# The last 48 columns of a routed expert's gated activations: rounded part and rest in one stationary tile

## The reference

```python
x = L0_attn_x                       # (4, 512, 256), f32
xn = _layernorm(x, axis=-1)
# experts: E, H, TOP_K = (8, 176, 2), ROUTED_SCALE = 2.5, xt = xn as rows
scores = jax.nn.sigmoid(xt @ gate_w.T)
top_scores, top_idx = jax.lax.top_k(scores, TOP_K)
top_scores = top_scores / (jnp.sum(top_scores, axis=-1, keepdims=True) + 1e-20) * ROUTED_SCALE
h = jnp.einsum('td,edh->eth', xt, w1)
u = jnp.einsum('td,edh->eth', xt, w3)
y = jnp.einsum('eth,ehd->etd', jax.nn.silu(h) * u, w2)
routed = jnp.einsum('etd,te->td', y, combine)       # combine: the two chosen scores of a row
shared = jax.nn.silu(xt @ sw1) * (xt @ sw3) @ sw2
x = x + attention(xn, wq, w_down, w_up, wo) + (routed + shared)
```

## Time and profile before

| | us |
|---|---|
| median of 3 runs | 741.92 |
| lowest, highest | 740.95, 744.02 |
| the profiled execution | 740.12 |
| its span, first to last instruction | 738.2 |

### The profile page before, as it was taken

One profiled execution on the slowest core, in us unless ns is written; L12 is line 12 of the kernel. 1 busy time (PEld: TensorE's weight loads), 2 busy tenths in 40 slices (PEclk: granted clock), 3 DMA queues, 4 the chain that ended last, 5 costly groups with the idle time before them and its releaser, 6 DMA issues.

```text
span 738.2 us, 15624 instructions
## 1 busy us (share of the span) xinstructions
PE 699.8 (95%) x4554; PEld 629.4 (85%) x4554; DVE 633.0 (86%) x1724; ACT 592.9 (80%) x1472; POOL 540.0 (73%) x497
## 2 busy tenths in 40 slices
PE   4788979999999999999999999999999999999985
PEld 3677777898898999999999999999999999988875
DVE  6677989999998889888988888898889888888885
ACT  3666667888878898888888888888888888888872
POOL 2544457788777778788888878787887788786890
PEclk9999999999999999999999999999999999999999
DMA  9552522443333455656456654655566545512103
GB/s 300 166 166 98 206 62 100 132 161 115 117 118 133 130 150 138 184 135 164 124 157 175 165 128 131 197 150 139 130 159 174 149 133 144 133 13 61 58 9 107
DMA packets 64899, 99.85 MB, mean 135 GB/s; under 512 B 9472, under 2 KB 38320, under 8 KB 64816
## 3 DMA queue, kind: packets, MB, share of 16 engines
q1 hardware_dynamic: 57664, 89.52, 39.1%
q0 software_dynamic: 7152, 9.34, 7.6%
HBM read 70.06 MB, written 28.78 MB: 134 GB/s over the span
## 4 chain that ended last, share of the span: by engine, by line
PE 71%; DVE 14%; ACT 5%; issue 4%; POOL 4%; DMA 1%; DVEq 0%; ACTq 0%; POOLq 0%
PE qk_proj L453 14%; PE u_acc L453 13%; PE scores L453 12%; PE ffn L453 10%; PE out_acc L453 10%; PE probs_t L556 7%; DVE acc L1261 2%; ACT swapped L768 2%; DVE rot L1206 2%; POOL rot L928 2%; POOL swapped L920 2%; DVE rot L1213 2%; DVE pt_lo L1237 1%; PE ffn L637 1%; PE ffn L611 1%
## 5 line engine op out<-in xcount | busy, mean ns | idle before, releaser
L920 POOL TENSOR_TENSOR swapped<-swapped,sin_t 128x512 f32<-128x512 f32 x128 | 167.7, 1310 | 140.8 <-DVE rot L1213 109.3
L935 POOL TENSOR_TENSOR qk_lo<-rot,qk_hi 128x512 fp32r<-128x512 f32 x128 | 163.3, 1295 | 8.5 <-ACT qk_hi L777 8.1
L1237 DVE TENSOR_TENSOR pt_lo<-probs_t,pt_hi 128x512 fp32r<-128x512 f32 x238 | 117.6, 494 | 48.7 <-ACT pt_hi L799 48.5
L788 ACT ACTIVATE probs<-scores,nbias 128x512 f32<-128x512 f32 (+3 forms) x256 | 135.1, 528 | 28.3 <-DVE nbias L1222 26.8
L768 ACT ACTIVATE swapped<-qk_proj 64x512 f32<-64x512 f32 x256 | 151.9, 593 | 6.1 <-PE qk_proj L453 1.4
L799 ACT ACTIVATE pt_hi<-probs_t 128x512 fp32r<-128x512 f32 x238 | 104.9, 441 | 42.8 <-PE probs_t L556 34.2
L1222 DVE CUSTOM_DVE_ANT_0 scores<-scores,mask 128x512 f32<-128x512 f32 (+3 forms) x256 | 125.2, 489 | 7.8 <-PE scores L453 1.5
L1261 DVE SCALAR_TENSOR_TENSOR acc<-out_acc,rsum,acc 128x256 f32<-128x256 f32 x256 | 111.0, 475 | 3.6 <-PE out_acc L453 1.8
L556 PE MATMUL probs_t<-ident,probs 128*128 128x128 f32 x604 | 105.4, 273 | 6.7 <-DVE pt_lo L1237 6.5
L1206 DVE TENSOR_TENSOR rot<-qk_proj,cos_t 128x512 f32<-128x512 f32 x128 | 87.4, 683 | 10.0 <-ACT swapped L768 9.2
L556 PEld LDWEIGHTS probs_t<-ident,probs 128*128 128x128 f32 x604 | 75.5, 140 | 22.5 <-issue 7.0
(11 more groups left out here) (181 smaller groups left out, 1907.8 us busy)
## 6 DMA issues: line engine op xcount, KB each, us to landing
wt<-expert_parts SPq DMA_DIRECT2D x39, 704.0 KB, 4.5
wt<-expert_parts SPq DMA_DIRECT2D x39, 512.0 KB, 3.9
raw_a<-in_attn SPq DMA_DIRECT2D x8, 768.0 KB, 5.2
xs_sorted<-u_lo SPq DMA_DIRECT2D x3, 1677.0 KB, 9.5
xs<-xs_sorted SPq DMA_DIRECT2D x39, 129.0 KB, 2.6
expert_parts<-split SPq DMA_DIRECT2D x8, 352.0 KB, 2.4
expert_parts<-raw_f SPq DMA_DIRECT2D x8, 352.0 KB, 2.4
ys_tokens<-mask SPq DMA_DIRECT2D x1, 2176.0 KB, 7.5
```

The costliest lines, as they stand in the source:

```text
L788: ac.activation(probs[:, m % 2, PR_AT[i]:PR_AT[i] + n], s_bank[i % 2][:, 0:n], ACT.Exp, bias=nbias[:, m % 2, i:i + 1], scale=-1.0, accum_o ...
L920: pool.tensor_tensor(swapped[:, which, :], swapped[:, which, :], sin_t[:, :], ALU.mult).then_inc(sinm_ok[which], 1)
L935: pool.tensor_tensor(qk_lo[:, m % 2, which, :], rot[:, which, :], f32(qk_hi[:, m % 2, which, :]), ALU.subtract).then_inc(rlo_ok[which], 1)
L1237: ve.tensor_tensor(pt_lo[:, c], turn_bank(m, j)[:, 0:n], f32(pt_hi[:, c]), ALU.subtract).then_inc(ptlo_ok, 1)
```

## The change

For routed tiles alone the second chunk is packed. VectorE writes the last 48 columns of g twice, to columns 128 to 175 and again to 192 to 239, so that after the transposes rows 0 to 47 and rows 64 to 111 hold the same values. ScalarE writes g_hi's second chunk only in rows 64 to 127; its rows 0 to 63 are cleared once by GpSimd before the first routed tile. VectorE's subtraction, which is the same instruction as before, then leaves in g_lo's second chunk the value itself (rounded on being written, as hi would be) in rows 0 to 63 and the rest in rows 64 to 127. The weights' last 48 rows are loaded twice too, to rows 0 to 47 and 64 to 111. One pass over the packed tile with the rounded weights gives hi x hi and lo x hi, a second with the weights' rests gives hi x lo, and in addition lo x lo. Five passes take the place of six; shared tiles keep six. ScalarE waits for GpSimd's clearing at the first routed tile, GpSimd for the last shared tile's output before it clears.

```diff
--- before.py
+++ after.py
@@ -43,6 +43,8 @@
 UP = 2 * HID
 W13, W2C = KD * UP, 2 * D
 FCOLS = W13 + W2C
+
+REST, HALF = HID - P, P // 2
 PART = [slice(0, W13), slice(W13, FCOLS)]
 
 F32 = mybir.dt.float32
@@ -254,7 +256,7 @@
         RAW_DMAS = [0]
         for e in (E, *range(E)):
             RAW_DMAS.append(RAW_DMAS[-1] + 2 * len(cuts(e * HID, HID, 2 * P)))
-            RAW_DMAS.append(RAW_DMAS[-1] + sum(len(cuts(e * HID + n, m, P)) for n, m in ((0, P), (P, HID - P))))
+            RAW_DMAS.append(RAW_DMAS[-1] + sum(n * len(cuts(e * HID + a, m, P)) for n, a, m in ((1, 0, P), (2, P, REST))))
         RAW_DMAS = RAW_DMAS[2:]
 
         def part_steps(s):
@@ -316,7 +318,9 @@
                     first, rows = e * HID + c * P, min(P, HID - c * P)
                     for a, z in cuts(first, rows, P):
                         src = ffn_d[a // (2 * P)][a % P:a % P + z - a, W2 + a // P % 2 * D:W2 + a // P % 2 * D + D]
-                        sp.dma_start(raw_f[a - first:z - first, W13 + c * D:W13 + c * D + D], src).then_inc(ld_raw, 16)
+                        for row in (0, HALF)[:c + 1]:
+                            sp.dma_start(raw_f[row + a - first:row + z - first, W13 + c * D:W13 + c * D + D],
+                                         src).then_inc(ld_raw, 16)
 
             for b in range(B):
                 sp.dma_start(acc[:, NT * b:NT * b + NT, :],
@@ -644,9 +648,17 @@
                 pe.wait_ge(glo_ok, f + 1)
                 if t is not None:
                     pe.wait_ge(ld_w2, 16 * (t + 1))
-                w = [(wt[:, 0, W13 + c * D:W13 + c * D + D], wt[:, 1, W13 + c * D:W13 + c * D + D]) for c in range(2)]
-                x = [(g_hi[:, c * P:c * P + P], g_lo[:, c * P:c * P + P]) for c in range(2)]
-                product(f_bank[:, 0:D], list(zip(x, w)), True, True).then_inc(y_ok, 1)
+                if t is None:
+                    w = [(wt[:, 0, W13 + c * D:W13 + c * D + D], wt[:, 1, W13 + c * D:W13 + c * D + D]) for c in range(2)]
+                    x = [(g_hi[:, c * P:c * P + P], g_lo[:, c * P:c * P + P]) for c in range(2)]
+                    product(f_bank[:, 0:D], list(zip(x, w)), True, True).then_inc(y_ok, 1)
+                    return
+                w = [wt[:, i, W13:W13 + D] for i in range(2)]
+                product(f_bank[:, 0:D], [((g_hi[:, 0:P], g_lo[:, 0:P]), w)], True, False)
+
+                pe.matmul(f_bank[:, 0:D], g_lo[:, P:2 * P], wt[:, 0, W13 + D:FCOLS], start=False, stop=False)
+                pe.matmul(f_bank[:, 0:D], g_lo[:, P:2 * P], wt[:, 1, W13 + D:FCOLS], start=False,
+                          stop=True).then_inc(y_ok, 1)
 
             def batch_rows(s):
                 b = pro_batch(s)
@@ -825,7 +837,13 @@
                     return
                 need(ac, y_ok, f)
                 ac.wait_ge(gt_ok, f + 1)
-                ac.activation(g_hi[:, :], f_bank[:, 0:2 * P], ACT.Copy).then_inc(ghi_ok, 1)
+                if routed(f) is None:
+                    ac.activation(g_hi[:, :], f_bank[:, 0:2 * P], ACT.Copy).then_inc(ghi_ok, 1)
+                    return
+                if routed(f) == 0:
+                    ac.wait_ge(zero_ok, 4)
+                ac.activation(g_hi[:, 0:P], f_bank[:, 0:P], ACT.Copy)
+                ac.activation(g_hi[HALF:P, P:2 * P], f_bank[HALF:P, P:2 * P], ACT.Copy).then_inc(ghi_ok, 1)
 
             def result(f):
                 t = routed(f)
@@ -1007,6 +1025,10 @@
                     scatter(n)
                 result_home(ffn_tile(s - 1))
                 row_homes(ffn_tile(s + 1))
+                if s == GAPS[-1]:
+
+                    pool.wait_ge(y_ok, STILES)
+                    pool.memset(g_hi[0:HALF, P:2 * P].bitcast(U32), 0).then_inc(zero_ok, 1)
                 for group in ADDS.get(s, ()):
                     add_routed(group, s)
                 if s == -LEAD + 1:
@@ -1288,12 +1310,18 @@
                     return
                 ve.wait_ge(gated_ok, f + 1)
                 need(ve, gt_ok, f)
-                ve.tensor_tensor(g[:, 0:HID], gated[:, :], f_bank[:, HID:UP], ALU.mult).then_inc(g_ok, 1)
+                last = ve.tensor_tensor(g[:, 0:HID], gated[:, :], f_bank[:, HID:UP], ALU.mult)
+
+                if routed(f) is not None:
+                    last = ve.tensor_tensor(g[:, P + HALF:P + HALF + REST], gated[:, P:HID],
+                                            f_bank[:, HID + P:UP], ALU.mult)
+                last.then_inc(g_ok, 1)
 
             def g_parts(f):
                 if f is None:
                     return
                 ve.wait_ge(ghi_ok, f + 1)
+
                 ve.tensor_tensor(g_lo[:, :], f_bank[:, 0:2 * P], f32(g_hi[:, :]), ALU.subtract).then_inc(glo_ok, 1)
 
             def add_shared(f):
```

## The result

The changed kernel takes 736.84 us (median of 4 runs, 735.76 to 738.02), the kernel before in the same comparison 741.43 us. The ratio is 0.9932, with a 95% interval of 0.9918 to 0.9946: 0.7% faster. The forecast was 737.2 us, 4.68 us less than the kernel before; measured are 4.59 us less. The profiled execution has 736.77 us and a span of 734.9, against 740.12 and 738.2 before.

What follows compares the result with a forecast made beforehand. PE was taken to bind, full in the routed stretch; 39 removed passes at 0.120 us give 4.68 us, all additions counted as 0, so the median of 741.92 becomes 737.2 us. The range for 8 in 10 was 735.0 to 740.5.

Steps and rivals of the forecast that it cites:

- The price of the pass: PE's output passes in 39 routed tiles: one pass fewer, at 0.120 us each, gains 4.68 us.
- PE's stretch is full: PE from 240 to 650 us: busy throughout, no wait, all steps 10.56 us long, to become 10.44.
- VectorE's second product: 48-column product in each routed tile: 0.13 us (bounds 0 to 0.26), covered by PE margins of 0.68 us and more.
- ScalarE's two copies: g_hi copy split in two per routed tile: 0.32 us, 0.06 more (bounds 0 to 0.26), covered by idle time.
- rival A: Added slots reach PE in steps with extra work, its stretch is less full, or loads late: 739.6 to 741.9 us; chance 0.15.
- GpSimd and SyncE: One clearing at step 14 and 11 further DMAs of up to 48 KB: both taken as cost 0.
- Rival B: VectorE's added product delays u_lo past out_acc in routed steps, from 0.69 us added; 3.9 us slower, 745.8; chance 0.04.
- Rival C: On PE, the removed pass is worth its whole 0.283 us: 11.0 us gained, 730.9 us; chance 0.03.
- The signs: Wrong if PE waits for u_lo, g or rot, routed steps aren't 0.12 us shorter, or time before 235 us moves over 1.

Runs made afterwards that it cites:

- The halves exchanged: Changed kernel with ScalarE writing the rounded values to rows 0 to 63 of g_hi's second chunk, the other half cleared; ratio 0.9926, median 736.60 us.
- the additions alone: Changed kernel with the last pass issued twice in routed tiles, so six passes again; ratio 0.9996, routed stretch 405.80 us.
- the pass alone: Kernel before with one output pass left out in each routed tile and nothing added; ratio 0.9943, routed stretch 401.24 us.

## Why the prediction was right, step by step

**The price of the pass** held to the last digit: 0.120 us from the chain, 38 x 0.12 = 4.56 in the run that removes it alone. The twelve passes beside it in the earlier trace rows were the right scale, and so was setting the 0.283 us of the earlier trace rows aside. The Trainium skill's sustained spacings ("TensorE: Matmul & The Clock Gate", Back-to-back issue gap), 81 ns at 128 columns and 131 ns at 512, give an estimated 98 ns at 256 when drawn in a straight line (the prediction took 95), which would have made 3.7 us for the 38; this case has 4.56.

**PE's stretch is full.** In plain steps no wait, one step length, and each 0.12 us removed shortens the step by 0.12, down to 9.97: shown. The steps with attention weights were 11.42 us long already before; the prediction gave one length for all.

**VectorE's second product**: 0.12 us, taken as 0.13, covered. The margin to the transposes of g was read right in kind and too large by 0.13: 0.55 us of cover where I had 0.68. What I had wrong is the way of the delay. I read the stretch from 410.35 to 413.28 as one without a gap and let all behind the product come 0.13 later; but pt_lo had waited there for pt_hi, and u_lo and g_lo come no later than before. For the same reason the idle time ahead of the later pt_lo is 0.80 us in the changed kernel, not the 0.69 that was to show it.

**ScalarE's two copies are the step that failed.** I took 0.32 us from the slot of a 128-column copy and they hold the engine for 0.59, with qk_hi longer by 0.13 in the steps where pt_hi follows at once: 0.45 us in place of 0.06. The term was mis-sized: the slot of 0.16 was that of two operations that both start at partition 0, and the bounds of 0 and 0.26 did not hold it. Nor did I list the wait that it reaches. In the step with attention weights pt_hi doesn't stand idle, it follows its queue; VectorE's pt_lo comes right after it and PE's next transposes after that. In the kernel before, pt_lo ended at 275.81 us, and the weight load of these transposes started at 276.29: 0.48 us. Take off 0.45 on ScalarE, 0.12 because PE is there a pass sooner, and the 0.05 from an end to a start, and the load is 0.14 us late: about the 0.12 that were removed.

```profile
276.54 0.56 DVE L1259 TENSOR_TENSOR pt_lo<-probs_t,pt_hi 128x384 fp32r<-128x384 f32 x1 [0.75 <-ACT pt_hi L811]
```

```profile
276.98 0.28 PE L660 MATMUL ffn<-wt,g_lo 128*128 128x256 f32 x1
277.15 0.44 PE L560 MATMUL probs_t<-ident,probs 128*128 128x128 f32 x2
```

These are VectorE's and PE's timelines of the changed kernel. pt_lo ends at 277.10 us, the transposes start at 277.15, 0.17 us behind the last pass and not 0.12; the next matmul starts at 277.35, 0.20 us behind them, where it was 0.14 in the kernel before (276.39 and 276.53). Together 0.11 us. The list of waits doesn't show it, for the reason given in the prediction: a wait shorter than the overlap of two matmuls leaves PE "busy". Price: 5 x 0.12 = 0.6 us, so 4.1 in place of 4.68. That is rival A in kind ("steps with extra work"), at a quarter of its lower price of 2.3 us. The halves exchanged, which take 0.40 of the 0.45 away, give the 0.6 us back.

The Trainium skill's fixed cost per instruction ("VectorE: DVE Perf Modes", The TRN2 errata) gave an estimated 0.14 us for the second copy and 0.18 for the second product. Measured are 0.06 for the copy with its start at partition 0 and 0.33 at partition 64, and 0.12 for the product: neither figure is met.

**GpSimd and SyncE** cost nothing, as forecast: the shared stretch has 179.98 us with the additions alone, 180.00 before, and the gap with the clearing in it 29.34 and 29.35.

**Rival B** is right in kind, a late result of VectorE makes PE wait; but the result that is late first is g and not u_lo, and from 0.55 us added, not 0.69. With 1.02 us the kernel is slower by 12 us (417.57 against 405.80 in the routed stretch). The change adds 0.12. **Rival C** is out by the pass alone.

**The total.** The routed stretch and the last pass give 4.05 to 4.14 us, the medians 4.59. The rest is the start's spread and an end that is 0.4 to 0.5 us shorter in every kernel of the table that has the additions (91.37 against 91.81 with the additions alone). About 0.15 of that comes where the routed tiles stop and the remainder in the last write's landing (3.6 us from its issue to the end of the span before, 3.3 with the additions alone). I did not forecast it and its cause stays open. So it is in part luck that the total came so near: the 0.6 us lost in five steps and the 0.44 us gained at the end, both missing from the sum, nearly cancel.

**The signs.** By its own last paragraph the prediction would be wrong if routed steps were not shorter by 0.12 us, or if what lies ahead of 235 us moved by over 1 us. Five of the 38 steps were not shorter: that is the step that failed. What lies ahead moved by 1.19 us between the two profiles (1.06 and 0.13), but it moves by 1.9 between two executions of the unchanged kernel, so this sign was set tighter than single executions repeat.

## What to carry to other kernels

When one engine's stretch is full, price a removed instruction by its distance from start to start in the chain. Then look for the cover in the steps that carry extra work, not in the plain ones: it is there that a longer queue on a helper engine eats the gain, and the list of waits is blind to it below the overlap of two matmuls, while the step length is not. A helper engine hides its waits in the same way: compare the distances of its operations from a fixed one, before and after. Two experiments, the removal alone and the additions alone, told apart what whole runs, with 2 us of chance in their start, could not.

## What the runs showed of the hardware

- ScalarE: a copy that starts at another partition than the one ahead of it does not overlap with it. 64x128 behind 128x128 takes 0.16 us at partition 0 and 0.30 at partition 64; the next operation, back at partition 0, then holds the engine for 0.65 us in place of 0.52. In keeping with it, the two `swapped` copies of 64x512 in the kernel before (L768), which change halves in reading and in writing, start 0.61 us apart, with a length of 0.60. What is done on partitions other than 0 and 64 no run shows.
- From the end of VectorE's instruction to the start of a PE that waits for it 0.05 to 0.06 us pass (396.54 to 396.60, 277.10 to 277.15). PE's weight load begins 0.09 to 0.11 us ahead of the matmul, and a margin that is read to the matmul is that much too large.
- PE's clock at the start: the same program stands at the 2.4 GHz level from 14 to 18 us in one execution and at the 1.2 GHz level from 16 to 18 in another. The idle time just before does not tell which: it is 1.65 us both in the kernel before, with passes 0.23 us apart, and in the changed one, with 0.43. The time at the lower level goes with the starts of the twelve traces, from 3.4 us (31.16 and 31.24) to 12.8 us (34.62).
